# A decoder layer on one core: fifteen of a row's sixteen state sums move from VectorE to GpSimd

## What is computed

```python
def step(state, xs):
    d_t, B_t, C_t, u_t = xs
    dA = jnp.exp(d_t[..., None] * A)
    state = state * dA + (d_t * u_t)[..., None] * B_t[:, None, :]
    y_t = jnp.einsum('ben,bn->be', state, C_t)
    return (state, y_t)
_, ys = jax.lax.scan(step, state0, xs)
y = jnp.moveaxis(ys, 0, -1)
y = y + D[None, :, None] * u
y = y * jax.nn.silu(z)
```

## Time and profile before

| | |
|---|---|
| median of 3 runs | 1762.98 us |
| span of the profiled execution | 1759.8 us |
| busy in it: PE, DVE, ACT, POOL | 1436.2, 1245.9, 941.3, 499.0 us |
| state sums on DVE into y (L1512, 60) | 137.4 us |
| state scans (L1501, 64) | 283.1 us |
| state products and inputs (L1507, L1495, 64 each) | 146.6 and 146.5 us |
| sends (L1918, 128, those of the last row among them) | 267.8 us |

### The profile page before, as it was taken

The page is one execution under the profiler, slowest core; times in us unless marked ns, Lnnn a source line. Parts: engine busy times, 40 slices in busy tenths (PEclk is TensorE's granted clock), DMA queues, the critical chain, the costliest instruction groups (busy, mean ns, idle before and its releaser), DMA issues. The chain is left out here.

```text
span 1759.8 us, 25049 instructions
## 1 busy us (share of the span) xinstructions
PE 1436.2 (82%) x6762; PEld 1018.9 (58%) x6763; DVE 1245.9 (71%) x1543; ACT 941.3 (53%) x2428; POOL 499.0 (28%) x307
## 2 busy tenths in 40 slices
PE   4899888988988798898869879977863746899996
PEld 1577665446766453676755357765422535677774
DVE  5465898756699975767998468699885424667663
ACT  4666662457567335675743447766320424566662
POOL 0000000000028600000880000068301545666664
PEclk9799999989999998899989989999985878999998
DMA  6692132132332422142133124212601446999985
GB/s 236 254 262 85 40 116 85 48 97 61 97 85 65 125 73 70 45 144 72 40 98 120 50 72 124 93 38 51 206 22 52 113 110 146 224 234 241 236 204 69
DMA packets 128788, 202.45 MB, mean 115 GB/s; under 512 B 44984, under 2 KB 46473, under 8 KB 127552
## 3 DMA queue, kind: packets, MB, share of 16 engines
q1 hardware_dynamic: 75120, 86.70, 17.5%
q0 software_dynamic: 27840, 63.83, 14.9%
q10 hardware_dynamic: 25744, 50.87, 9.6%
HBM read 170.57 MB, written 46.21 MB: 123 GB/s over the span
## 5 line engine op out<-in xcount | busy, mean ns | idle before, releaser
L1918 POOL DMA_INDIRECT lists<-entry,slot x128 | 267.8, 2092 | 227.9 <-DVE slot L1686 190.2
L1501 DVE TENSOR_TENSOR_SCAN state<-decay,dbu 128x2048 f32<-128x2048 f32 x64 | 283.1, 4423 | 24.2 <-ACT decay L1051 22.9
L1914 POOL DMA_DIRECT2D wq<-wq_dram x30 | 21.5, 720 | 869.9 <-PE pair L581 744.2
L645 PE MATMUL bank<-v_aug,probs 128*128 128x129 f32 x2048 | 253.1, 283 | 8.1 <-ACT probs L1045 8.1
L645 PEld LDWEIGHTS bank<-v_aug,probs 128*128 128x128 f32 x2048 | 244.5, 198 | 17.2 <-ACT probs L1045 16.2
L755 PE MATMUL bank<-wout,o_t 128*128 128x512 f32 x512 | 236.1, 616 | 0.0
L1045 ACT ACTIVATE probs<-bank 128x512 f32<-128x512 f32 x256 | 145.8, 605 | 106.3 <-PE bank L627 93.3
L1051 ACT ACTIVATE decay<-delta,neg_a 128x511 f32<-128x511 f32 x256 | 164.8, 736 | 65.4 <-DVE state L1501 59.4
L755 PEld LDWEIGHTS bank<-wout,o_t 128*128 128x128 f32 x512 | 100.0, 199 | 122.5 <-issue 122.1
L1953 POOL DMA_INDIRECT out<-y_ring,add_ids x68 | 125.2, 1842 | 94.8 <-DMA out<-y_ring,add_ids 66.7
L1495 DVE TENSOR_TENSOR dbu<-du,b_bc 128x2048 f32<-128x2048 f32 x64 | 146.5, 2289 | 7.0 <-DMA c_bc<-bc_dram 5.2
(11 more groups left out here) (227 smaller groups left out, 2731.8 us busy)
## 6 DMA issues: line engine op xcount, KB each, us to landing
wq<-wq_dram POOLq DMA_DIRECT2D x30, 1024.0 KB, 8.6
w_raw<-in_w_exp ACTq DMA_DIRECT2D x32, 768.0 KB
wout<-in_wout SPq DMA_DIRECT2D x64, 256.0 KB, 2.8
b_bc<-bc_dram SPq DMA_DIRECT2D x64, 256.0 KB, 3.7
c_bc<-bc_dram SPq DMA_DIRECT2D x64, 256.0 KB, 4.6
w_raw<-in_w_exp ACTq DMA_DIRECT2D x32, 512.0 KB
lists<-in_const ACTq DMA_DIRECT2D x1, 8712.0 KB, 48.4
q_s<-in_x SPq DMA_DIRECT2D x4, 1024.0 KB, 8.1
```

Source lines behind the costliest of these rows:

```text
L645: mm = pe.matmul(bank_o[half][:, (t % 2) * (DH + 1):(t % 2 + 1) * (DH + 1)], probs[:, k, t * P:(t + 1) * P], v_aug[:, k, :], start=(k == 0 ...
L1501: dve.tensor_tensor_scan(state[:].rearrange("p e t -> p (e t)"), dA, dbu[:].rearrange("p e t -> p (e t)"), 0.0, ALU.mult, ALU.add).then_in ...
L1918: pool.indirect_dma_start(out=lists, out_offset=bass.IndirectOffsetOnAxis(ap=slot[:, t, k:k + 1].bitcast(U32), axis=0), in_=entry[:, t, :] ...
```

## The change

GpSimd adds states 0 to 14 of each row into `y`, a wait and a `tensor_tensor` each; VectorE keeps the last sum, into `y_end`. `dbu` and `state` become two places used by turns (even states in `dbu`, odd ones in `state`): input, scan and product of a state all work in place in one of them. So VectorE can go on with the next state while GpSimd reads the one before. New waits: the input of state n waits for the sum of state n - 2, the input of state 1 for `skip`, the last sum for GpSimd's 15th. On GpSimd the query weight loads and the sends are laid by hand between the sums: `load_wq(b, 2)` stands behind sum 1, `load_wq(b, 3)` behind sum 3, `load_wq(b + 1, 0)` behind sum 7 and its sends, `load_wq(b + 1, 1)` behind all; three sends of the row before follow each of sums 5 to 14, the last two come after that.

```diff
+        place = [dbu, state]
             def state_input(r, n):
                 i = n % 2
                 dve.wait_ge(S[f"bc_in{i}"], r * (DS // 2) * 32 + (n // 2 * 32 + 32))
-                dve.tensor_tensor(dbu[:], du[:], b_bc[:, i:i + 1, :].to_broadcast([P, ET, T]), ALU.mult).then_inc(S["dbu_ok"], 1)
+                if n == 1:
+                    dve.wait_ge(S["skip_ok"], r * ET + ET)
+                if n >= 2:
+                    dve.wait_ge(S["sum_ok"], summed(r, n - 2))
+                dve.tensor_tensor(place[i][:], du[:], b_bc[:, i:i + 1, :].to_broadcast([P, ET, T]), ALU.mult).then_inc(S["dbu_ok"], 1)
 
             def state_scan(r, n):
+                now = place[n % 2][:].rearrange("p e t -> p (e t)")
...
-                dve.tensor_tensor_scan(state[:].rearrange("p e t -> p (e t)"), dA, dbu[:].rearrange("p e t -> p (e t)"), 0.0,
-                                       ALU.mult, ALU.add).then_inc(S["scan_ok"], 1)
+                dve.tensor_tensor_scan(now, dA, now, 0.0, ALU.mult, ALU.add).then_inc(S["scan_ok"], 1)
 
             def state_product(r, n):
...
-                dve.tensor_tensor(dbu[:], state[:], c_bc[:, i:i + 1, :].to_broadcast([P, ET, T]), ALU.mult).then_inc(S["bc_free"], 1)
-            def state_sum(r, n, dst=y):
-                dve.wait_ge(S["bc_free"], r * DS + n + 2)
-                dve.tensor_tensor(dst[:], y[:], dbu[:], ALU.add).then_inc(S["y_ok"], 1)
-                dve.wait_ge(S["y_ok"], r * DS + n + 1)
+                dve.tensor_tensor(place[i][:], place[i][:], c_bc[:, i:i + 1, :].to_broadcast([P, ET, T]), ALU.mult).then_inc(S["bc_free"], 1)
+            def last_sum(r):
+                dve.wait_ge(S["bc_free"], r * DS + DS + 1)
+                dve.wait_ge(S["sum_ok"], summed(r, DS - 2))
+                dve.tensor_tensor(y_end[:], y[:], place[(DS - 1) % 2][:], ALU.add).then_inc(S["y_ok"], 1)
+                dve.wait_ge(S["y_ok"], r + 1)
...
+            def add_state(b, n):
+                pool.wait_ge(S["bc_free"], b * DS + n + 2)
+                if n == 0:
+                    pool.wait_ge(S["skip_ok"], b * ET + ET)
+                else:
+                    pool.wait_ge(S["sum_ok"], b * (DS - 1) + n)
+                pool.tensor_tensor(y[:], y[:], place[n % 2][:], ALU.add).then_inc(S["sum_ok"], 1)
+            def send_some(b, first, count):
+                if first == 0:
+                    pool.wait_ge(S["slot_ok"], b + 1)
+                    pool.wait_ge(S["lists_in"], 16)
+                for i in range(first, min(first + count, TT * TOPK)):
+                    send(i // TOPK, i % TOPK, S["sent"])
             wq_stored(pool)
-            for group in range(1, G):
-                load_wq(0, group)
-            for b in range(NB - 1):
-                for group in range(G):
-                    load_wq(b + 1, group)
-                wait_apart(pool, S["slot_ok"], b + 1)
-                pool.wait_ge(S["lists_in"], 16)
-                for t in range(TT):
-                    for k in range(TOPK):
-                        send(t, k, S["sent"])
+            load_wq(0, 1)
+            for b in range(NB):
+                add_state(b, 0)
+                add_state(b, 1)
+                load_wq(b, 2)
+                for n in range(2, 4):
+                    add_state(b, n)
+                load_wq(b, 3)
+                add_state(b, 4)
+                for n in range(5, DS - 1):
+                    add_state(b, n)
+                    if b > 0:
+                        send_some(b - 1, (n - 5) * 3, 3)
+                    if n == 7 and b < NB - 1:
+                        load_wq(b + 1, 0)
+                if b > 0:
+                    send_some(b - 1, (DS - 6) * 3, TT * TOPK)
+                if b < NB - 1:
+                    load_wq(b + 1, 1)
```

More of the change, by code:

```diff
@@ L275, in decoder_layer @@
             exp_ok dA_ok oT_ok oc_ok sz_ok fT_ok rexp_ok
-            dve_step bn_ok ag_ok nw ln_x wqlo_ok wkvlo_ok xlo_ok klo_ok qlo_ok conv_ok kn_ok q_ok scan_ok bc_free o_ok on_ok x1_ok zr_ok ys_ok x2_ok xf_ok dbu_ok den_ok y_ok chain
+            dve_step bn_ok ag_ok nw ln_x wqlo_ok wkvlo_ok xlo_ok klo_ok qlo_ok conv_ok kn_ok q_ok scan_ok skip_ok sum_ok bc_free o_ok on_ok x1_ok zr_ok ys_ok x2_ok xf_ok dbu_ok den_ok y_ok chain
             lgs_ok act_ok slot_ok
@@ L1486, in skip, with summed @@
                 for e in range(ET):
-                    dve.tensor_scalar(y[:, e, :], state[:, e, :], d_skip[:, e:e + 1], None, ALU.mult)
+                    dve.tensor_scalar(y[:, e, :], state[:, e, :], d_skip[:, e:e + 1], None, ALU.mult).then_inc(S["skip_ok"], 1)
                 dve.memset(dA3[:, :, 0:1], 0.0).then_inc(S["dve_step"], 1)
                 dve.wait_ge(S["dve_step"], r + 2)
+            def summed(r, n):
+                return r * (DS - 1) + n + 1
             def state_input(r, n):
@@ L1531, in later_heads @@
                             state_product(r, n)
-                            state_sum(r, n)
                         if group == 2 and j == 3:
@@ L1544, in last_states @@
                         dve.wait_ge(S["wout_used"], b * (H - 1) + 8)
-                    state_sum(b, n, y_end if n == DS - 1 else y)
+                        last_sum(b)
                     if n < DS - 1:
@@ L1605, in gated @@
             def gated(b):
-                dve.wait_ge(S["y_ok"], b * DS + DS)
+                dve.wait_ge(S["y_ok"], b + 1)
                 for t in range(TT):
@@ L1706, in start_heads @@
                 denominators(row, 1)
-                state_sum(row, 0)
                 q_norm(at.job("g1a"))
@@ L1714, in start_heads @@
                     gated(b)
-                state_sum(row, 1)
                 q_norm(at.job("g1b"))
@@ L1735, in start_heads @@
                 q_norm(at.job("g2a"))
-                state_sum(row, 2)
                 state_input(row, 3)
@@ L1743, in start_heads @@
                 q_norm(at.job("g2b"))
-                state_sum(row, 3)
                 if tail:
@@ L1754, in start_heads @@
                 state_product(row, 4)
-                state_sum(row, 4)
                 state_input(row, 5)
```

## The result

The changed kernel takes 1846.72 us (median of 4 runs, 1838.82 to 1850.55) against 1762.85 for the one before: ratio 1.047, 95% interval 1.0425 to 1.0507. It is slower by 84 us; 1836 was forecast, and a range of 1765 to 1872. The profiled execution has a span of 1837.0 us, 77.2 more than before. Ratios leave out two executions that ran slow: one of the kernel before (1785.71 us) and one of experiment 9's second kernel (3516.64 us).

What follows compares the result with a forecast made beforehand. VectorE was taken to set the pace in states 4 to 11 of each row, PE elsewhere. 48 + 9 + 9 + 2 + 6 = +74 us on the profiled 1759.8 gave 1834, stated as a median of 1836, range 1765 to 1872.

Steps and rivals of the forecast that it cites:

- GpSimd holds VectorE: Wherever VectorE's next instruction reads two SBUF tiles, it waits until GpSimd's addition ends; assumed, the sends showing only the reverse.
- The length: One addition on GpSimd was taken as 4.42 us, like VectorE's scan, with ends of 2.29 and 5.18 us.
- The full stretch: States 4 to 11, VectorE full: seven intervals grow from 11.50 to 13.55 us, +12.0 us a row, +48 in four.
- The cycle of 14.6 us: GpSimd's queue, states 5 to 14 of rows 2 to 4: an addition and three sends take 14.6 us, against 13.55.
- little of it shows before state 11: GpSimd's queue lags 1 us more per state against one interval's slack, so only +2 us a row, +6 (0 to 15).
- (c): Rival: VectorE is held and GpSimd's queue becomes the pace in three rows, +20 to +30 us, 1860; chance 0.12.
- (d): The forecast itself: VectorE is held for the whole addition, range 1805 to 1865 us; chance 0.65.
- The start of a row: States 0 to 4: addition 1 holds the gate and `q_norm` behind it, +3 us in three rows, +9.
- Beside the output projection: States 12 to 15: additions 13 and 14 delay the keys' norm and `q_norm`, +3 us in three rows, +9 (0 to 12).
- The end: Last row, behind the projection: three intervals of +2 us, partly taken by 1.89 us to spare, +2 in all.
- (a): Rival: GpSimd waits for VectorE but never holds it, additions run beside the scans, 43 us gained, 1720; chance 0.13.
- (b): Rival: VectorE is held briefly or cheaply, additions near 2.3 us, gains and costs cancel, 1757 to 1775 us; chance 0.10.

Runs made afterwards that it cites:

- experiment 9's second kernel: Kernel before with the two places, no addition on GpSimd, VectorE adding state 11 behind head 15's denominators; ratio to the kernel before 1.001 (0.998 to 1.004).
- Experiment 7: Two places, VectorE adding, but nobody adds states 4 to 10 and the expert part's output additions wait for each other; full stretches 80.1, 83.4, 83.5, 83.4 us.
- 2: Two places with all sums on VectorE; beside them GpSimd writes zeros into a spare tile, two memsets per state; span 1757.2 us.
- 3: Two places with all sums on VectorE; GpSimd copies each state's tile in two halves, input n + 2 waiting for that; span 1819.9 us.
- 4: Changed kernel, but for states 0 to 14 GpSimd adds channel tiles 0 and 1 and VectorE tiles 2 and 3; span 1794.4 us.
- experiment 5: Changed kernel with no sends between the sums, all 32 of a row behind GpSimd's 15th sum; median 1829.29 us, ratio to the kernel before 1.032.
- experiment 8: Changed kernel, but VectorE adds states 1 and 14 at their old places; 1834.2 us, ratio to the kernel before 1.036 (1.028 to 1.043).

## Why the prediction was right, point by point

**What bounds the kernel: right.** Experiment 7 shows VectorE's pace in the full stretch.

**GpSimd holds VectorE: right, and the reason is reading.** The prediction took this from sends that wait for VectorE, and assumed the other direction. The scan of 8.60 us shows it, and 2, 3 and 4 show what does it. The Trainium skill, SBUF — State Buffer, section Who interferes with whom, has GpSimd contend with a two-input VectorE instruction when it reads SBUF and not when it only writes; the memset and the copy agree (nothing at nine starts of the gate's instructions, and 0.66 to 0.72 us).

**The length: 4.42 was taken, 4.50 to 4.60 is what an addition takes that waits for nothing.** The Trainium skill, GPSIMD Engine Reference, section Performance versus the Vector engine, gives 4497 ns; the shortest here is 4504.

**The full stretch: 54 us forecast (48 of hold, 6 of queue), 49.0 measured, by two errors that cancel.** The hold was too dear: row 1, which has no sends, is +8.5 us and not +12.0. Per addition VectorE loses 3.9 us ((8.5 + 8 x 2.33) / 7) and not 4.37; one of the seven stands behind a weight load (addition 7, then `load_wq(1, 0)`, then addition 8 falls on an input and holds it 3.3 us only). Four rows make 34 in place of 48. The queue was too cheap: 4.8 us a row by experiment 5, 14.4 in all, in place of 6, and with the last row's end (4.9) it is 19.3. That the two errors cancel is luck. The cycle of 14.6 us was right to 0.1; the step that failed is "little of it shows before state 11". Rival (c), the queue as the pace, was right on the mechanism in rows 2 to 4, and its sign, inputs that wait for the sum, was in the trace. So the case is (d), the forecast, with (c) on top, and only the hold that was priced too high kept the sum near. (c) was too dear at 20 to 30 on top of the 6: the queue costs 19.3 in all.

**The start of a row: 9 forecast, 11.5 measured, for a partly wrong reason.** The gate was named; `q_norm` was named only behind the gate. It is held by addition 0 as well, and that is worth more (1.6 of the 3.8 us a row by PE's waits, the gate 1.1 to 1.2).

**Beside the output projection: 9 forecast, 11.6 measured.** Addition 14 holds the query norm's first instruction there (676.16, 3.46 us, 0.16 before), as the prediction said. What that costs is not shown: experiment 8 leaves addition 14 out, and row 1 gains 4.1 us there, rows 2 and 3 together nothing. **The end: 2 forecast, 5.1 measured.** To the last `slots` it is 7.1: 2.2 from the additions, as forecast, and 4.9 from the queue, which the prediction left out there; the expert part is 2.0 shorter.

**The median: 3 us above the span were added, 9.7 are there** (1846.7 and 1837.0). The profiled execution is the fastest of the four (1838.82), the others take 1844.75 to 1850.55. No trace of those is there; in the other traces it is the expert part that differs by such amounts. That and the stages make the 11 us between 1836 and 1847.

Rivals (a) and (b) fell: scans did not keep 4.42 us, and in the full stretch the holds last nearly as long as an addition. One sign failed too: PE was to be busy below 70% there, and is at 72% in row 1 and 71% in row 2.

## What to carry to other kernels

Work moved from VectorE to GpSimd is not off VectorE's path if it reads SBUF: count the GpSimd instruction's own length as time of VectorE wherever the next VectorE instruction reads two SBUF operands, even one of 8 columns, and compare it with what was removed (4.2 against 2.3 here). It is free only where VectorE waits anyway or runs instructions with one operand in SBUF or one in PSUM (norm statistics beside addition 11 keep 2.45 us, denominators 0.23), or where nobody waits for what is held. And a queue that gets a new duty brings its old ones along: three sends behind each addition made GpSimd the pace of later states in three rows, which its busy share over the span did not tell. Last, a stage that varies by itself, as the expert part here, hides effects of a few us in the whole time; compare stage by stage.

## What the runs showed of the hardware that was not expected

A GpSimd copy with one SBUF operand holds VectorE too (0.66 to 0.72 us for a copy of 1.03), a memset does not (953 ns, 945 to 962; the gate keeps 2.49 us beside it and takes 4.17 beside the copies). A VectorE instruction of 0.17 us can take 4.43. VectorE's busy time went up though 60 instructions of it were gone. And 2.4 us won in row 2 were lost again to TensorE's clock (0.73 in place of 0.89 in one window of 15 us).
